# How the slots' results come back: three reloads behind the last store, over all 128 partitions

## The reference, cut to what matters

```python
y = jnp.einsum('btd,bst->bsd', xn, dispatch_w)                 # slot inputs
y = gelu(jnp.einsum('sio,bsi->bso', fc1_weight, y) + fc1_bias)
y = jnp.einsum('sio,bsi->bso', fc2_weight, y) + fc2_bias       # slot results
out = jnp.einsum('bsd,bst->btd', y, combine_w)                 # mixed per token
h = layernorm(h + out)
```

## Time and profile before

| | us |
|---|---|
| median of 3 runs | 1305.57 (1305.18 to 1306.07) |
| the profiled execution, its own time | 1307.93 |
| its span, first to last instruction | 1306.2 |
| mean granted TensorE clock, as a share of 2.4 GHz | 0.947 |

### The profile page before, as it was taken

One profiled execution on the slowest core, in us unless ns is written; L12 is line 12 of the kernel. 1 busy time (PEld: TensorE's weight loads), 2 busy tenths in 40 slices (PEclk: granted clock), 3 DMA queues, 4 the chain that ended last, 5 costly groups with the idle time before them and its releaser, 6 DMA issues.

```text
span 1306.2 us, 34037 instructions
## 1 busy us (share of the span) xinstructions
PE 1200.2 (92%) x12578; PEld 962.2 (74%) x12578; DVE 782.9 (60%) x2049; ACT 708.3 (54%) x1613; POOL 572.3 (44%) x878
## 2 busy tenths in 40 slices
PE   5999999999999999999999999999996999995553
PEld 4788888888888888888888888888873555553332
DVE  4566666666666666666666666666673222221797
ACT  5456666666666666666666666666653111110476
POOL 4355454555545554545555455545442000000564
PEclk8999999999999999999999999999995999998655
DMA  4411211111111112111111111121071899995686
GB/s 140 183 39 60 79 61 49 49 49 49 49 49 49 49 57 77 63 49 49 49 49 49 49 49 49 57 78 62 13 270 58 352 422 420 421 389 124 190 263 188
DMA packets 50246, 158.33 MB, mean 121 GB/s; under 512 B 5292, under 2 KB 31266, under 8 KB 37794
## 3 DMA queue, kind: packets, MB, share of 16 engines
q1 hardware_dynamic: 32610, 145.04, 30.9%
q10 hardware_dynamic: 17600, 12.78, 3.2%
HBM read 132.18 MB, written 25.62 MB: 121 GB/s over the span
## 4 chain that ended last, share of the span: by engine, by line
PE 74%; DVE 16%; issue 5%; ACT 1%; POOL 1%; DVEq 1%; SPq 1%; DMA 0%; ACTq 0%; POOLq 0%
PE ps L914 9%; PE ps L915 8%; PE ps L916 7%; DVE p_sb L778 7%; PE ps L973 7%; PE ps L944 6%; PE ps L1008 6%; PE ps L1178 5%; PE ps L1195 4%; PE ps L1051 3%; PE ps L956 3%; PE ps L957 2%; DVE res L887 2%; PE ps L991 2%; PE ps L1074 2%
## 5 line engine op out<-in xcount | busy, mean ns | idle before, releaser
L413 POOL TENSOR_TENSOR xl<-x_sb,xh 128x392 fp32r<-128x392 f32 x192 | 189.1, 1019 | 86.6 <-DVE gn L753 78.7
L778 DVE TENSOR_TENSOR p_sb<-ps,dec 98x1176 f32<-98x1176 f32 x128 | 177.0, 1383 | 56.4 <-PE ps L973 56.4
L973 PE MATMUL ps<-qm,kT 32*98 32x196 f32 x1536 | 117.0, 343 | 9.7 <-DVE p_sb L778 7.6
L717 DVE BATCH_NORM_STATS2 st<-ps 98x6 f32<-98x192 f32 x128 | 40.0, 355 | 130.8 <-PE ps L944 130.8
L1008 PE MATMUL ps<-p_sb,vpad 98*32 98x98 f32 x3072 | 112.7, 251 | 1.5 <-DVE p_sb L778 1.5
L636 ACT ACTIVATE hg<-ps 128x768 f32<-128x768 f32 x32 | 26.0, 812 | 159.0 <-PE ps L1200 159.0
L1008 PEld LDWEIGHTS ps<-p_sb,vpad 98*32 98x32 f32 x3072 | 84.7, 109 | 35.0 <-issue 24.6
L973 PEld LDWEIGHTS ps<-qm,kT 32*98 32x98 f32 x1536 | 75.2, 158 | 35.2 <-DVE p_sb L778 23.1
L944 PE MATMUL ps<-wo,og 96*98 96x192 f32 x512 | 93.7, 325 | 0.0
L879 DVE COPY y2st<-ps 128x192 f32<-128x192 f32 x32 | 11.4, 358 | 136.1 <-PE ps L1178 128.7
L1224 PE MATMUL ps<-y2b,cbuf 64*98 64x192 f32 x256 | 48.2, 526 | 44.6 <-POOL y2b L513 44.6
(11 more groups left out here) (175 smaller groups left out, 3390.4 us busy)
## 6 DMA issues: line engine op xcount, KB each, us to landing
x_sb<-in_xT SPq DMA_DIRECT2D x32, 1176.0 KB, 5.7
w1v<-in_fc SPq DMA_DIRECT2D x32, 1152.0 KB, 8.2
w2v<-in_fc SPq DMA_DIRECT2D x32, 1152.0 KB, 10.8
h_dram<-h SPq DMA_DIRECT2D x32, 294.0 KB
h2r<-h_dram SPq DMA_DIRECT2D x32, 294.0 KB
out<-o_sb ACTq DMA_DIRECT2D x32, 294.0 KB
comb_dram<-cst SPq DMA_DIRECT2D x32, 98.0 KB, 1.8
cbuf<-comb_dram SPq DMA_DIRECT2D x32, 98.0 KB, 4.0
```

Of the source, the lines that this page charges most:

```text
L413: pool.tensor_tensor(xl[:, k], x_sb[:, k], xh[:, k].bitcast(F32), ALU.subtract)\
L778: dve.tensor_tensor(dst, src, rate.unsqueeze(2).to_broadcast([T, PAIRS, 2, TOK]), ALU.mult)\
L973: mm = pe.matmul(ps[0:T, SC_AT + r, mt * TOK:(mt + 1) * TOK].rearrange("p (b n) -> p b n", b=2), kT[rows, g, n], qm[rows, g, :, n], start= ...
```

## The change

The row blocks are replaced by blocks of pairs of images. SP waits for every store of `y2_dram`, and then issues three transfers, each to all 128 partitions: pairs 0 to 3, 4 to 11, and 12 to 31. A row of one transfer is 4, 8 or 20 pairs of one slot and image, so 3,072, 6,144 or 15,360 contiguous bytes. Each transfer has its own semaphore. POOL waits for the first, adds the bias of pairs 0 to 3, waits for the other two, and goes on into its loop. SP's earlier wait on `fc2_mm`, which kept the first block off the weights that lie where `y2r` goes, is gone.

```diff
-READY = (NU - RING, NU - REST, NU)
+PARTS = ((0, DEEP), (DEEP, 3 * DEEP), (3 * DEEP, NP))
...
-        y2r_loaded = sem("y2r_loaded")
+        y2r_loaded = [sem(f"y2r_loaded{n}") for n in range(len(PARTS))]
...
-            sp.wait_ge(fc2_mm, RING * TURNS - 2)
-            for u0, u1 in zip((0,) + READY[:-1], READY):
-                for m in range(Y2):
-                    sp.wait_ge(y2_stored[m], 16 * ((u1 - m + Y2 - 1) // Y2))
-                for a in range(2):
-                    rows = slice(64 * a + 2 * u0, 64 * a + 2 * u1)
-                    sp.dma_start(y2r[rows, :, :], y2_dram[2 * u0:2 * u1, a]).then_inc(y2r_loaded, 16)
+            for m in range(Y2):
+                sp.wait_ge(y2_stored[m], 16 * ((NU - m + Y2 - 1) // Y2))
+            for (p0, p1), there in zip(PARTS, y2r_loaded):
+                sp.dma_start(y2r[:, p0:p1, :], y2_dram[:, :, p0:p1, :].rearrange("s a p d -> a s (p d)"))\
+                    .then_inc(there, 16)
...
-            pool.wait_ge(y2r_loaded, 32 * len(READY))
+            pool.wait_ge(y2r_loaded[0], 16)
             for n in range(DEEP):
                 bias(n, n)
+            for there in y2r_loaded[1:]:
+                pool.wait_ge(there, 16)
             with pool.Fori(0, NP // DEEP - 1) as w:
```

## The result

The changed kernel takes 1351.55 us (median of 4 runs, 1349.05 to 1352.26) where the kernel before, run beside it, takes 1305.38 us (4 runs, 1304.90 to 1306.07): a ratio of 1.035, with an interval of 1.0332 to 1.0368. It is 46.2 us slower. 1346.7 us was predicted, with a range of 1341 to 1362.

The account below looks back on a forecast made before the run. Phase 3 was taken to wait for the complete `y2r` reload, then DVE to set the pace at 2.6 us a pair. DVE's first shift moving from 1218.45 to 1259.6 us adds 41.1 to 1305.57: 1346.7 us, range 1341 to 1362.

Parts of the forecast that it names:

- On how many engines: Reload transfers: 2 DMA engines each, the largest number up to 16 dividing both sides' outermost counts, 128 and 2.
- How fast one engine is: Reload: 26.4 GB/s an engine, bounds 26.4 and 9.3; slow are several engines that write neighbouring partitions together.
- The early reload goes: End of phase 2: without its traffic the late store's pause goes; last `y2st` ends at 1194.7 us, 4.2 us earlier.
- The last store: Last `y2_dram` store before the reload: lands in 1.6 us, bound 4.0; SP is free at 1196.3 us.
- Start, completion and data: Reload: 2.4 us fixed, bound 3.2; data 7.4 + 14.9 + 37.2 = 59.6 us; all there at 1258.3 us.
- So the early first part hides nothing.: Start of phase 3: first part there at 1206.1 us, but DVE waits for POOL, which waits for the third part.
- 5 us until DVE needs them: Behind the reload: loads of pairs 4 to 6 queue behind the third part, with 5 us to spare; DVE's pace stays.
- The sum: DVE's first shift of phase 3 moves from 1218.45 to 1259.6 us: +41.1 us on the median 1305.57, giving 1346.7 us.
- the terms listed for 2 engines: Full-rate case, chance 0.83: slow fc2 +1.5, store +2.4, fixed part +0.8, engine rate 2.5 either way, remaining pause +2.7 us.

Follow-up runs that it names:

- Run 1: Changed kernel with each of the three reload parts sent as two transfers of 64 rows, outermost count 64 on both sides: 1304.04 us, ratio 0.9986 to the kernel before.
- run 2: Changed kernel with each part in two 64-row halves, each cut into 62 and 2 rows, twelve transfers: 1354.51 us, ratio 1.0389 to the kernel before.
- run 5: Changed kernel with `y2_dram` laid out image outermost, four stores of 32 rows a step, reloads 128 rows on both sides: 1299.25 us, ratio 0.9951 to the kernel before.
- run 8: Changed kernel with `y2_dram` image outermost, four stores a step, and one reload transfer for all 32 pairs: 1304.25 us, ratio 0.9987 to the kernel before.
- Run 4: Kernel before without its early reload: one block of all rows, two transfers of 64 partitions behind the last store: 1310.45 us, ratio 1.0043 to the kernel before.
- Run 3: Changed kernel with POOL's waits for parts two and three moved to the biases of pairs 4 and 12: 1348.78 us, ratio 1.0325 to the kernel before.
- run 6: Changed kernel with `y2_dram` image outermost and POOL's later waits at the biases of pairs 4 and 12: 1297.19 us, ratio 0.9932 to the kernel before.

## Why the prediction was right, and where it was off

**On how many engines.** Right, and it is what decides. Two small packets and 53 GB/s show it in the changed kernel. Run 1 takes the count of 2 away and with it 47 us; run 2 keeps the halves, gives them a count of 62, and has two engines and the time back.

**How fast one engine is.** The value was right: parts two and three, 2.75 MB, come in 1257.82 - 1204.59 = 53.2 us, 25.9 GB/s for an engine against 26.4 taken. The reason was not. "Slow are several engines that write neighbouring partitions together" is not what the runs show: in runs 5 and 8 16 engines write neighbouring partitions at the full rate. Slow are many engines into one half of the partitions (runs 4 and 8): some 205 GB/s is what 64 partitions take, whether 16 engines share it (runs 1 and 4, 13 GB/s each) or 13 (14.6 GB/s, 190 together). The slower reloads of 4 and 8 rows weren't tried by themselves.

**The early reload goes.** Right in kind and size. `y2st` ends 4.57 us behind the start of the last transposes (1187.64 to 1192.21); forecast were 4.6. Run 4 shows that the early reload alone was the cause.

**The last store** took 1.62 us, as 1.6 was forecast, and the reload was issued 6.27 us behind the transposes (6.2 forecast).

**Start, completion and data.** From the issue to the first bias 10.68 us went by and not 9.8, from the issue to POOL's release 63.9 and not 62.0. These 2 us were within the bounds given. Half of them lie ahead of the first bias, the other half are the two engines' 2% below the rate taken; what lowers it wasn't tested.

**"So the early first part hides nothing."** True of the changed kernel, but POOL's wait is only the first of two reasons. Run 3 takes it away and gets 2 or 3 us, since the loads of the pairs after the first ones stand behind the third part on its two engines. The prediction named these loads only at the end, as having "5 us until DVE needs them". With 16 engines the early first part is worth 5.0 us (run 8 against 5), and the waits at need 2.1 us more by the medians (run 6 against 5), of which the two profiled seams show 0.9.

**The sum.** The forecast of 1346.7 us lies 4.8 us low. 2.0 of them are the start and the data above (a seam of 71.5 us against a forecast of 1259.6 - 1190.07 = 69.5), 0.4 are the end (88.15 against 87.75 us). The rest is a step of arithmetic: +41.1 us was worked out against an execution 2.4 us above the median, and then added to the median. That execution was slow because of its store wait and the fc2 behind it, and the change removes both in any case; so the gain from them was counted 2 us too high for a typical run. The table gives it: 1305.57 less some 1279.4 is a typical seam of 26.2 us, and 71.6 - 26.2 = 45.4, with the 0.4 of the end 45.8 us, where 45.5 and 46.2 were measured. One thing stays open. Both profiled executions of the changed kernel, at 1349.05 and 1349.76 us, are at the low end of its runs and 1.6 us shorter outside the seam than before's; none near its median of 1351.55 was profiled, so that their time outside the seam is 1279.4 too is inferred and not seen. The traces do show that these two start differently: between 20 and 35 us TensorE's mean granted clock is 0.89 of 2.4 GHz in them and 0.77 in the other ten profiled executions. The change does not bring this, since runs 1 to 3 have the changed kernel's program up to the seam, and have 0.77. The 0.12 of 15 us are 1.8 us of work at the full clock, an estimate that fits the 1.6; but run 1, 1278.37 us outside the seam at 0.77, shows that the clock there is not all of it.

The prediction also had a value for the profiled execution, 1349.0 us, and 1349.05 was measured. That this fits so closely is luck: its seam is 2.0 us longer than forecast, and the rest 2.0 us shorter than in the execution that the forecast started from. As for the range, the terms listed for 2 engines reach from 2.5 us below the sum to 9.9 above it, so from 1344.2 to 1356.6 us and not from 1342 to 1355; the measured time lies inside both.

## What to carry to other kernels

Before merging transfers into one, write down the outermost count of both sides: in every transfer counted here the engines are the largest number up to 16 that divides both, and it can be the DRAM side's layout that decides, as 2 and 62 did here. If it is the layout, change it where the data are written (in run 5 the four stores of 32 rows put the reload 7.49 us behind the last transposes instead of 6.27, and the kernel was still 6.3 us faster than before). And when a profiled execution lies off the median, find out which wait makes it so before a gain from that wait is counted against the median.

## What the runs showed of the hardware that was not expected

Sixteen engines that write 64 partitions move 201 to 209 GB/s, and 412 to 435 GB/s into 128, with rows of the same length: here a reload into one half of the partitions took twice as long for its bytes.

A long transfer on two engines holds up what SP issues behind it. The `comb` load that SP took 0.37 us to issue before took 8.02 us in the changed kernel, and an `h2r` load of run 3 took 18.52 us. The timeline of the changed kernel has the issue, and the transfers of 1207 to 1222 us give the time to landing (the last column, a median of two):

```profile
1207.11 8.02 SPq L352 DMA_DIRECT2D cbuf<-comb_dram  x1
cbuf<-comb_dram SPq DMA_DIRECT2D x2, 98.0 KB, 45.5
```

It was 2.7 us before. The packets show why. The first line is of the transfers of 1214 to 1217 us of the changed kernel, when the first of these loads moves, the second of 1255.5 to 1262 us, when the reload ends:

```profile
DMA packets 152, 0.25 MB, mean 83 GB/s; under 512 B 14, under 2 KB 126, under 8 KB 152
DMA packets 103, 0.21 MB, mean 33 GB/s; under 512 B 12, under 2 KB 60, under 8 KB 99
```

In the first, 14 small packets and 112 rows (126 - 14) have gone, where a whole `comb` load has 16 and 128: fourteen engines are through with it at once. In the second come 48 more rows (60 - 12), the last 16 of each of three such loads, which the two engines of the reload had kept back. One short share on a busy engine makes a load that runs on sixteen as late as the slowest of them.
